# Holding back five convolution units of output channel tile 1, and reloading image 0 into slots whose pieces have been stored

## The reference, cut to what matters

```
a  = sign(x2)                                  # what the block's binary activation gives forward
y  = conv2d(a, alpha * sign(w), 3x3, pad 1)
mu, var = mean and variance of y over (N, H, W), per output channel
out = (y - mu) / sqrt(var + 1e-5) * gamma + beta + x2
```

## Time and profile before

| | |
|---|---|
| time, median of 3 runs | 1985.28 us (1984.22 to 1986.18) |
| the profiled execution's own time | 1984.29 us |
| its span, first to last instruction | 1982.5 us |
| granted TensorE clock, mean | 0.976 of full speed |
| PE, DVE, ACT, POOL busy | 1908.3, 1567.9, 1420.2, 1211.2 us |
| end of PE's last product | about 1933 us after the span's start |
| HBM read, written | 84.48 MB, 33.62 MB |

### The profile page before, as it was taken

One profiled execution on the slowest core, in us unless ns is written; L12 is line 12 of the kernel. 1 busy time (PEld: TensorE's weight loads), 2 busy tenths in 40 slices (PEclk: granted clock), 3 DMA queues, 4 the chain that ended last, 5 costly groups with the idle time before them and its releaser, 6 DMA issues. The chain is left out here.

```text
span 1982.5 us, 40003 instructions
## 1 busy us (share of the span) xinstructions
PE 1908.3 (96%) x15232; PEld 1638.3 (83%) x15232; DVE 1567.9 (79%) x2151; ACT 1420.2 (72%) x2793; POOL 1211.2 (61%) x848
## 2 busy tenths in 40 slices
PE   7999999999999999999999999999999999999990
PEld 2799999998998899998999999988998999864440
DVE  5777787788877877788877777788887887767787
ACT  5777777777777777778777777778777777652335
POOL 4556555667855555567755556677665556468760
PEclk6899999999999999999999999999999999999995
DMA  6111111012211111012111110112111102434009
GB/s 213 41 51 60 53 39 35 32 64 64 69 46 59 61 40 32 32 68 95 58 56 62 40 31 25 56 54 63 32 32 32 32 30 77 156 120 162 1 39 385
DMA packets 58287, 133.67 MB, mean 67 GB/s; under 512 B 9328, under 2 KB 9328, under 8 KB 57584
## 3 DMA queue, kind: packets, MB, share of 16 engines
q1 hardware_dynamic: 58096, 131.10, 19.4%
HBM read 84.48 MB, written 33.62 MB: 60 GB/s over the span
## 5 line engine op out<-in xcount | busy, mean ns | idle before, releaser
L760 POOL CAST Ph<-P 128x1024 fp32r<-128x1024 f32 x496 | 725.9, 1464 | 625.2 <-ACT P L518 625.2
L610 DVE TENSOR_REDUCE nb<-scw 128x1 f32<-128x512 f32 (+1 forms) x988 | 680.9, 690 | 288.6 <-PE scw L408 283.6
L529 ACT ACTIVATE scw<-scw,nb 128x512 f32<-128x512 f32 (+1 forms) x988 | 655.7, 664 | 317.6 <-DVE nb L610 317.3
L426 PE MATMUL accb<-Ph,xh 64*128 64x512 f32 x2048 | 807.6, 394 | 1.3 <-ACT tb L539 1.3
L426 PE MATMUL acct<-Ph,xh 64*128 64x512 f32 x2048 | 804.9, 393 | 0.0
L426 PE MATMUL accb<-Ph,xl 64*128 64x512 f32 x2048 | 800.7, 391 | 0.0
L426 PE MATMUL acct<-Ph,xl 64*128 64x512 f32 x2048 | 796.8, 389 | 0.0
L620 DVE TENSOR_TENSOR Pl<-P,Ph 128x1024 fp32r<-128x1024 f32 x512 | 664.4, 1298 | 27.3 <-ACT Ph L523 15.9
L426 PE MATMUL acct<-Pl,xh 64*128 64x512 f32 x2048 | 635.7, 390 | 0.0
L426 PE MATMUL accb<-Pl,xh 64*128 64x512 f32 x2048 | 632.2, 388 | 0.0
L518 ACT ACTIVATE P<-ee 128x1024 f32<-128x1024 f32 x512 | 526.1, 1028 | 82.2 <-PE ee L399 66.1
(11 more groups left out here) (166 smaller groups left out, 1390.9 us busy)
## 6 DMA issues: line engine op xcount, KB each, us to landing
wk<-xt SPq DMA_DIRECT2D x32, 512.0 KB, 3.8
xres<-x SPq DMA_DIRECT2D x32, 512.0 KB, 3.8
x<-xres SPq DMA_DIRECT2D x32, 512.0 KB, 2.8
R<-rd SPq DMA_DIRECT2D x32, 256.0 KB, 3.1
xn<-x SPq DMA_DIRECT2D x16, 512.0 KB, 12.6
xr<-x SPq DMA_DIRECT2D x16, 512.0 KB, 10.5
out<-xr SPq DMA_DIRECT2D x16, 512.0 KB, 10.1
An<-x SPq DMA_DIRECT2D x14, 512.0 KB, 5.2
```

The costliest lines, as they stand in the source:

```text
L426: return pe.matmul(to[:, :], w[rows, g * GM + k, c * 128:(c + 1) * 128], p[rows, s, k * QC:(k + 1) * QC], start=g == 0 and i == 0, stop=g ...
L529: nc.scalar.activation(to, to, ACT.Exp, bias=nb[:, t % 2, w:w + 1], accum_out=bsum[:, t % 2, w:w + 1]).then_inc(bsum_done, 1)
L610: nc.vector.tensor_reduce(nb[:, t % 2, w:w + 1], of, AX.X, ALU.max, negate=True).then_inc(nmax_done, 1)
L760: nc.gpsimd.tensor_copy(Ph[:, e % RP, :], P[:, e % 2, :]).then_inc(ph_done, 1)
```

## The change

Five units of channel tile 1 are held back instead of three: the order ends (11,0), (12,0), (13,0), (14,0), (15,0), (14,1), (11,1), (12,1), (13,1), (15,1). So five transformed inputs must be kept, in five slots: `An`, `Bn`, two new tiles `Vn0` and `Vn1`, and the end of `Yv`. `LAST0` is 26. The signs of unit S are now made ahead of place (8(S-2)+4)//5, a unit each 1.6 places, instead of one each second place.

All twelve pieces of images 1 to 3 of channel tile 0 are made between the last five outputs, 7 by POOL and 5 by DVE, dealt out by the table `DEALT`. The pieces of image 0, tile 0, come next, then tile 1 of images 1 to 3, then image 0, tile 1. Image 0 is reloaded into the places in `xr[1]` and `xr[2]` whose pieces have been stored: after the store of piece n (n from 3 to 10) SP waits until store n-3 has landed (`left[n - 3]`) and issues load n-3 there. The scratch area reserved for transfers is set to 1024 bytes, which makes room. At i = 27 the first of the two row writes waits for all four planes instead of three, since it writes where unit 14's fourth plane lies.

```diff
-        V = [v_view(An), v_view(Bn), v_view(Yv[:, late:late + VLEN].bitcast(BF16))]
+        V = [v_view(An), v_view(Bn)] + [v_view(sb(f"Vn{k}", [128, VLEN], BF16)) for k in range(KEPT - 3)]
+        V.append(v_view(Yv[:, late:late + VLEN].bitcast(BF16)))
...
-        places = [(U, o) for U in range(NU - 3) for o in range(CT)]
-        places += [(NU - 3, 0), (NU - 2, 0), (NU - 1, 0), (NU - 2, 1), (NU - 3, 1), (NU - 1, 1)]
+        places = [(U, o) for U in range(NU - KEPT) for o in range(CT)]
+        places += [(U, 0) for U in range(NU - KEPT, NU)]
+        places += [(U, 1) for U in (NU - 2, NU - 5, NU - 4, NU - 3, NU - 1)]
         NP = len(places)
-        LAST0 = NP - 4
+        LAST0 = NP - KEPT - 1
+        SIGNS = {(8 * (S - 2) + 4) // 5: S for S in range(2, NU)}
+        pieces = [(b, 0, k, xr[SLOT[b]][:, 0, k * PIECE:(k + 1) * PIECE]) for b in (1, 2, 3) for k in range(UN)]
+        EARLY = len(pieces)
+        homes = [pieces[h][3] for h in range(2 * UN)]
+        pieces += [(0, 0, k, homes[k]) for k in range(UN)]
+        pieces += [(b, 1, k, xr[SLOT[b]][:, 1, k * PIECE:(k + 1) * PIECE]) for b in (1, 2, 3) for k in range(UN)]
+        pieces += [(0, 1, k, homes[UN + k]) for k in range(UN)]
+        POOLED = (0, 2, 3, 5, 7, 8, 10)
+        DEALT = {LAST0 + 1: range(0, 2), LAST0 + 2: range(2, 5), LAST0 + 3: range(5, 8),
+                 LAST0 + 4: range(8, 10), LAST0 + 5: range(10, 12)}
...
             for n, (b, c, k, r) in enumerate(pieces):
-                if n == 4:
-                    sp.wait_ge(m_filled, (NP - 1) * VK)
-                    load_home(0)
-                    load_home(1)
-                if n == 7:
-                    sp.wait_ge(m_filled, NP * VK)
-                    sp.wait_ge(r_pool, len(POOLED))
-                    for h in range(2, 2 * UN):
-                        load_home(h)
...
+                if 0 <= n - 3 < len(left):
+                    sp.wait_ge(left[n - 3], 16)
+                    load_home(n - 3)
...
-                if U >= 3:
-                    pool.wait_ge(m_filled, (U - 2) * (VK * CT))
+                if U >= KEPT:
+                    pool.wait_ge(m_filled, (U - KEPT + 1) * (VK * CT))
...
-                if i == LAST0 + 1:
-                    scale_add(1)
-                if i == LAST0 + 2:
-                    scale_add(4)
+                for n in DEALT.get(i, ()):
+                    if n not in POOLED:
+                        scale_add(n)
```

## The result

| | before | changed |
|---|---|---|
| time, median of 5 runs | 1985.65 us (1984.22 to 1986.18) | 1975.79 us (1972.71 to 1976.99) |
| ratio to before | | 0.9947, 95% interval 0.9936 to 0.9958 |
| span of the profiled execution | 1982.5 us | 1970.9 us |
| `BN_AGGR` of channel tile 0, tile 1 | 1919.29, 1938.26 | 1908.14, 1938.51 |
| DVE's last row of `scale_add` begins | 1940.50 | 1941.12 |

The change makes the kernel 0.53% faster, 9.9 us by the medians.

What follows compares the result with a forecast made beforehand. Taken as bound: the unbroken transfers at the end. Earlier start -8.2 us, two pieces less -2.5, load loss 6.3 in place of 2.3: -6.7 us, giving a median of 1978.6 us; range 1974.0 to 1983.5.

Steps and rivals of the forecast that it cites:

- M: Transfer time lost where image 0's loads run between stores: taken as 6.3 us, own range 2.3 to 8.9, against 2.3 before.
- the mixed stretch: Tail transfers where loads of image 0 alternate with stores, 17 pieces: 290 to 350 GB/s until about 1949, then 419.
- What bounds the kernel: At the end, the transfers set the time: when they become full, how many pieces remain, what is lost; not DVE.
- PE's order at no cost: Reordered units on PE end where they did; POOL's transformed inputs are ready in time, with 12.4 us in hand.
- Second statistics 2.3 us later: Tile 1's statistics at 1940.6 against 1938.26, after five outputs (19.2 us) and five `scale_add` (10.3 us) on DVE.
- After them: After tile 1's statistics: coefficients 2.24 us, a shift 0.3 us more, DVE's row from 1943.1, its 20 pieces ending at 1967.1.
- The beginning of the unbroken stretch, -8.2 us, and two pieces less in it, -2.5 us: Tail transfers become full at 1921.4 instead of 1929.6, with 37 pieces left instead of 39, at 1.251 us each.
- DVE covered, 3.9 us in hand: Transfers busy until 1949.0, the last row's first store there at 1945.1, so DVE's 2.3 us of delay cost nothing.
- A: Rival: each turn between loads and stores costs the whole 1.29 us, so 1981.5 to 1982.6 us, no change; chance 0.14.
- B: Rival: loads amid stores go at 205 GB/s, as at the convolution's start, so slower, 1994.5 us; chance 0.07.
- C: Rival: DVE becomes the bound, all five `scale_add` meeting a POOL piece at its start; 1981.2 us; chance 0.05.
- D: Rival: PE waits for transformed inputs, making both statistics 10.4 us later; 1989.0 us; chance 0.04.

Runs made afterwards that it cites:

- e8_reload_only: Kernel before with only the reload of image 0 moved behind stores 3 to 10; three units held back, seven early pieces: 1985.68 us, ratio 1.0000.
- e4_early7: Changed kernel with only 7 pieces made ahead of the second statistics, the other 25 after them: 1982.95 us, ratio 0.9988.
- e6_last: Changed kernel with all eight loads of image 0 in a row behind store 11: 1983.18 us, ratio 0.9990.
- e2_noload: Changed kernel with the 8 loads of image 0 left out, so part of the output is wrong: 1972.83 us, ratio 0.9938.
- e3_delay: Changed kernel with six more statistics instructions on DVE ahead of the second statistics: 1977.64 us, ratio 0.9961.
- e5_fours: Changed kernel with the loads of image 0 in two rows of four, after stores 6 and 10: 1978.31 us, ratio 0.9963.

## Why the prediction was right, point by point

The measured time, 1975.8, lies in the range and 2.8 us under the forecast of 1978.6; faster had a chance of 0.72. The direction and the mechanism came out, the size did not: the sum named 6.7 us and the stage shortened by 10.9. That the median lies well inside the range is in part luck: with the loss as measured, the prediction's own sum gives 1974.0 to 1974.3, under the 1974.6 that it gave as the low end of M, and at the edge of the wider range. The median moved by 9.9 us and not 10.9, with the spread that comes from ahead of the convolution. Two of the prediction's signs failed as well: the mixed stretch was to run at 290 to 350 GB/s up to 1949 and ran at 273, 385 and 418, and the last store was to be issued at about 1968 or later and was issued before 1966.

*What bounds the kernel.* Right for the kernel before: e8_reload_only keeps the beginning of the full stretch and has no gain, while e4_early7 and e6_last leave the first statistics where the change put them and lose 7.7 and 9.1 us, mostly by gaps in the transfers. For the changed kernel it is only half of it: DVE's row bounds as well, 0.5 to 0.8 us behind (e2_noload, e3_delay).

*PE's order at no cost.* Right: PE's last product ends 162.8 us after the convolution's start in each of the kernels.

*First statistics 10.47 us earlier.* Right: 149.2 to 138.8 in the table.

*Second statistics 2.3 us later.* They came 0.9 us later, counted from the start of the convolution. The five outputs are right; the five `scale_add` took 1.27, 1.89, 1.89, 3.04 and 1.27 us, and from the start of each to the start of what follows 9.0 us in all, where the prediction had 10.3. The three in the middle each began while a piece of POOL was under way and took what was left of it (0.8, 0.8 and 2.0 us) and another 1.1 us. So the price is set by where in POOL's piece they begin, and the mean of two cases was a guess.

*After them.* Right: 2.6 us from the second statistics to DVE's row, which makes 20 pieces in 24.0 us.

*The beginning of the unbroken stretch, -8.2 us, and two pieces less in it, -2.5 us.* Right: the transfers are full from 1921 in the profile. -10.7 us in all for these two terms.

*The loss M at the loads.* This is the term that was mis-sized: 6.3 us, with the middle taken between 5.2 and 7.4. Measured 1.4 + 0.3 = 1.7 us. The bound below, 2.3, was nearest. With M = 1.7 the same sum gives -11.3 us, and -11.0 with the 0.3 us that the last stores lost; the stage gave -10.9. The step that failed is that the loss goes by the load or by the rate of the pair. The runs show it where loads meet a queue that has just been idle or is thin (1.1 to 2.3 us, at the first loads of the stretch, again at the second row of e5_fours and at the first four loads of e8_reload_only), and next to none at single loads in a full queue. The row of six in the kernel before lost 1.0 us in a full queue, so loads in a row may cost there; that wasn't tried apart.

*DVE covered, 3.9 us in hand.* Wrong by the same term: the transfers held the end 4.6 us less long. DVE's row was also ready about 1.2 us earlier than forecast, and 0.5 to 0.8 us of cover was left.

*SP's queue.* Right: SP waited for a store to land ahead of a load once, for 0.7 us.

*Rivals.* A (a loss for each turn) is refuted: eight turns cost 1.7 us, one turn in e6_last 2.3. B likewise: 273 GB/s in the worst stretch of 4 us of the changed kernel, and only there; the prediction's estimate of 2 us for each load, worked out from the Trainium skill (DMA: Bandwidth & Descriptors, Latency and other measured facts), gives 16 us, and the trace has 1.7. C didn't occur: one `scale_add` of 3.04 and two of 1.89. D didn't: unit 15's input was there 12.4 us early.

## What to carry to other kernels

When the tail is a full queue of transfers, ask when the queue begins to be full and what is left to put in it; the statistics of channel tile 0 two units of PE time earlier (10.5 us) shortened the stage by 10.9 us. Holding work back pays only if the time that it opens is filled: without the five further pieces seven tenths of the gain were gone. Loads that must be done anyway belong in the gaps between early stores, one by one, as soon as a place is free; the same eight loads in a row behind the early stores made the stage 9 us longer. And when the queue gets shorter, look at what is just behind it: here DVE's row, 0.5 to 0.8 us away, so that a further gain has to come from both.

## What the runs showed of the hardware that I had not expected

- Single loads of 512 KB between stores ran at 418 GB/s, the rate of stores alone (419), once the queue was full: five of the eight in the changed kernel, and the last four of e8_reload_only at 415. Where the queue had just been idle or was thin, loads and stores together lost 1.1 to 2.3 us: at the first loads of each run that had loads, also in a kernel that made a small load 4.6 us ahead, again after a rest (e4_early7: 181 GB/s at a share of 0.76 in 1942 to 1948), and at the second row of e5_fours (1.3 us). Why is open. That the queues are nearly empty there is what the cases have in common; it wasn't tried apart.
- A DVE instruction on one column took 2.34 us, 0.16 elsewhere, beside a 2.36 us piece of POOL that had begun 0.03 us before it. The Trainium skill (SBUF — State Buffer, Who interferes with whom) has a DVE instruction with two SBUF inputs contend with a GpSimd instruction that reads SBUF; it calls the port pair that they share an exclusive lock, and says that the order of issue and not the shape of the operation decides who waits. The rows agree, also with the `scale_add` of 3.04 us at 1930.53, where a piece of POOL (2.35 us) had begun at 1930.14.
- The convolution began between 1769.2 and 1773.7 us in the profiled executions, with nothing changed ahead of it. Part of that is there early: one and the same store of the attention is issued at 163.55 in the changed kernel and at 166.65 in e4_early7, whose convolution begins 4.3 us later.

```profile
163.55 0.40 SPq L318 DMA_DIRECT2D x<-xres  x1
```

```profile
166.65 0.39 SPq L318 DMA_DIRECT2D x<-xres  x1
```

Where it comes from is open.
